# One of twelve C products of a selective scan moved from VectorE to GpSimd, and a residual matmul moved one group later

## The reference, cut to what matters

```python
def selective_scan(xs, dts, As, Bs, Cs, Dsk):
    ...
    def step(h, inp):
        u_t, d_t, B_t, C_t = inp
        dA = jnp.exp(d_t[..., None] * As)
        h = h * dA + (d_t * u_t)[..., None] * B_t[:, :, None, :]
        y = jnp.einsum('bkcn,bkn->bkc', h, C_t)
        return (h, y)
    ...
...
y = out_y[:, 0] + inv_y[:, 0] + wh_y + invwh_y
...
y = (y - mu) / jnp.sqrt(var + 1e-05) * out_norm_g + out_norm_b
y = y * jax.nn.silu(z)
return y @ out_proj_w.T
...
x = x + _L1_conv_ref(_gn(x), ...)
```

## Time and profile before

| quantity | value |
|---|---|
| median of 3 runs | 3176.9 us (3176.43 to 3177.23) |
| the profiled execution's own time | 3180.68 us |
| its span in the profile | 3177.8 us |
| granted TensorE clock, mean of the span | 0.99 |
| DVE busy in the whole span | 2619.3 us |
| POOL busy in the whole span | 2155.6 us |
| first scan of the last stage starts | 1019.93 us |

### The profile page before, as it was taken

The page is one execution under the profiler, slowest core; times in us unless marked ns, Lnnn a source line. Parts: engine busy times, 40 slices in busy tenths (PEclk is TensorE's granted clock), DMA queues, the critical chain, the costliest instruction groups (busy, mean ns, idle before and its releaser), DMA issues.

```text
span 3177.8 us, 101351 instructions
## 1 busy us (share of the span) xinstructions
PE 2769.4 (87%) x39496; PEld 2074.0 (65%) x39496; DVE 2619.3 (82%) x4161; ACT 1823.4 (57%) x3872; POOL 2155.6 (68%) x1814
## 2 busy tenths in 40 slices
PE   4999999999996788888888888888888888888876
PEld 4999999996664555656656566565665656656554
DVE  6444444445776999999999999999999999999985
ACT  1211211212224777777777777777777777777763
POOL 5333333330003988889888898888988889888883
PEclk9999999999998999999999999999999999999999
DMA  5000000002334554554545545455454554545541
GB/s 203 0 0 0 0 0 0 0 0 80 114 113 136 155 165 150 166 171 144 177 144 166 176 143 176 143 166 178 141 175 143 168 179 139 174 143 170 178 124 47
DMA packets 57086, 385.29 MB, mean 121 GB/s; under 512 B 10101, under 2 KB 15061, under 8 KB 31701
## 3 DMA queue, kind: packets, MB, share of 16 engines
q1 hardware_dynamic: 57044, 384.79, 39.2%
HBM read 352.64 MB, written 32.11 MB: 121 GB/s over the span
## 4 chain that ended last, share of the span: by engine, by line
POOL 35%; issue 28%; PE 25%; DVE 8%; ACT 2%; DMA 1%; POOLq 1%; SPq 0%; ACTq 0%; DVEq 0%
POOL arena L489 22%; PE ps L1096 10%; PE ps L1105 9%; POOL arena L462 3%; POOL arena L476 3%; POOL arena L471 3%; POOL arena L466 3%; DVE arena L772 2%; DVE arena L769 2%; PE ps L1092 2%; DVE conv_out L201 1%; PE ps L1149 1%; POOL arena L454 1%; DVE stats L565 1%; PE ps L1078 1%
## 5 line engine op out<-in xcount | busy, mean ns | idle before, releaser
L1228 PE MATMUL ps<-arena,ident 128*128 128x392 f32 (+1 forms) x4096 | 1163.0, 417 | 0.9 <-DVE arena L781 0.9
L947 ACT ACTIVATE ps<-arena,abias,a 128x390 f32<-128x390 f32 x1024 | 689.3, 677 | 314.9 <-DVE arena L772 177.1
L1228 PEld LDWEIGHTS ps<-arena,ident 128*128 128x128 f32 x4096 | 683.0, 191 | 144.1 <-DVE arena L781 1.2
L781 DVE TENSOR_TENSOR arena<-arena,ps 128x784 f32<-128x784 f32 x768 | 745.8, 971 | 26.6 <-PE ps L1218 0.3
L769 DVE TENSOR_TENSOR_SCAN arena<-ps,arena 128x392 f32<-128x392 f32 x768 | 703.2, 957 | 23.3 <-POOL arena L489 22.8
L772 DVE TENSOR_TENSOR_SCAN arena<-ps,arena 128x392 f32<-128x392 f32 x768 | 703.3, 957 | 0.0
L1218 PE MATMUL ps<-arena,sel 96*128 96x196 bf16 x3072 | 392.1, 250 | 321.1 <-DVE arena L781 321.0
L1218 PEld LDWEIGHTS ps<-arena,sel 96*128 96x128 bf16 x3072 | 230.3, 98 | 626.5 <-DVE arena L781 594.3
L489 POOL TENSOR_TENSOR arena<-arena 128x784 f32<-128x784 f32 x256 | 474.4, 1853 | 128.8 <-PE ps L1228 126.4
L951 ACT ACTIVATE ps<-arena,abias,a 128x195 f32<-128x195 f32 x1024 | 474.7, 504 | 140.0 <-DVE arena L769 72.7
L489 POOL TENSOR_TENSOR arena<-arena,wh_sb 128x784 f32<-128x784 f32 x256 | 472.8, 1853 | 69.0 <-PE ps L1228 66.9
(11 more groups left out here) (172 smaller groups left out, 3142.0 us busy)
## 6 DMA issues: line engine op xcount, KB each, us to landing
wx_sb<-b_by_state SPq DMA_DIRECT2D x64, 1568.0 KB, 6.3
wh_sb<-b_by_state SPq DMA_DIRECT2D x64, 1568.0 KB, 6.2
arena<-b_by_image SPq DMA_DIRECT2D x128, 784.0 KB, 9.1
arena<-x_seq SPq DMA_DIRECT2D x4, 2352.0 KB, 16.1
x_in<-x_pair SPq DMA_DIRECT2D x16, 588.0 KB, 4.2
x_dram<-x SPq DMA_DIRECT2D x16, 588.0 KB, 2.8
x<-x_dram SPq DMA_DIRECT2D x16, 588.0 KB, 9.9
out<-xhat SPq DMA_DIRECT2D x16, 588.0 KB, 2.8
```

Source lines behind the costliest of these rows:

```text
L781: dve.tensor_tensor(h, h, bank(3), ALU.mult).then_inc(s["readout_ready"], 1)
L947: ins = act.activation(r, src, ACT.Exp, scale=a01[:, c:c + 1], bias=abias01[:, c:c + 1])
L1228: mm = pe.matmul(ps[:, 5 if g < 8 else 6, 0:cols], ident[:, :], h[:, m * cols:(m + 1) * cols], start=(opens and m == 0), stop=(closes and ...
```

## The change

Of group 7 (`POOL_READS`) the product with C is taken from DVE's `read_out` and given to POOL as `pool_read`. POOL does it behind drive 10 of the same station (`READ_LEAD` = 3), in place in the ring buffer, when both scans of group 7 are done. It reads C from an SBUF tile, `c_chunk`, which is filled for each station by a DMA broadcast from DRAM (`spread_c`); `spill_b` writes the two states' rows there (two DMAs more). PE leaves out the spread of group 7: in the slot of group 7 it spreads group 8, in that of group 8 nothing. The sum of group 7 is done in the slot of group 10 (`BEHIND` = 2), after that of group 9, once `pool_read` is done; `ORDER` holds the order of the sums, by which `drive` now knows how many sums free its buffer. Semaphores `c_ready` and `readout_ready` rise by 2 at the group ahead of 7, so that the counts stay those of the groups. ACT's `read_bc` waits for the C spills too. Separately, the output projection's matmuls of (2, 6) move to (2, 5), and each residual matmul stands in the group next to its projection, at (2, 6), (3, 5) and (3, 7).

The diff, cut to its core:

```diff
...
 CHUNK = 16 * T
+POOL_READS = (7,)
+READ_LEAD = 3
+BEHIND = 2
 EPS = 1e-5
...
     b_by_image = nc.dram_tensor("b_by_image", [K4, 2, N, T], F32)
+    c_by_state = nc.dram_tensor("c_by_state", [K4, len(POOL_READS), 2, 2, T], F32)
     with ExitStack() as ctx:
...
         ident = sb("ident", [128, 128])
+        c_chunk = sb("c_chunk", [128, len(POOL_READS) * GC])
         sel = sb("sel", [96, N, 3, 128], BF16)
...
             "oproj_ready", "o_ready", "out_stored", "fin_z", "fin_x1",
-            "b_spilled", "b_chunk0", "b_chunk1", "b_chunk2", "skipped")}
+            "b_spilled", "b_chunk0", "b_chunk1", "b_chunk2", "skipped",
+            "c_spilled", "c_chunk_in", "pool_read")}
         convs = ((pad01, conv01_out, 2 * H + 1, par01, s["conv01_step"]), (pad2, conv2_out, H, par2, s["conv2_step"]))
...
                     lambda a: a.rearrange("p (m q t) -> p m q t", m=2, q=2))
+        def reduce_order():
+            order, late = [], []
+            for g in range(GRP):
+                if g in POOL_READS:
+                    late.append(g)
+                else:
+                    order.append(g)
+                order += [r for r in late if r + BEHIND == g]
+            return order
+        ORDER = reduce_order()
         def half_cols(hf):
...
                 sp.dma_start(b_by_image[k].rearrange("i n t -> (i n) t"), xdbl[0:2 * N, 0:T]).then_inc(s["b_spilled"], 16)
+                for q, g in enumerate(POOL_READS):
+                    for img in range(2):
+                        sp.dma_start(c_by_state[k][q, :, img, :], xdbl[N * img + 2 * g:N * img + 2 * g + 2, T:T2]
+                                     ).then_inc(s["c_spilled"], 16)
             def spread_b(P, k, j, first=False):
...
                                      ).then_inc(s["b_chunk2"], 16)
+            def spread_c(P, k, first=False):
+                sp.wait_ge(s["c_spilled"], (P + 1) * (32 * len(POOL_READS)))
+                if not first:
+                    sp.wait_ge(s["pool_read"], P * len(POOL_READS))
+                rows = c_by_state[k].rearrange("q n i t -> (q n i t)").unsqueeze(0)
+                sp.dma_start(c_chunk[:, :], rows.broadcast_to([128, len(POOL_READS) * GC])).then_inc(s["c_chunk_in"], 16)
             spill_b(0, 0)
...
                 spread_b(0, 0, j, True)
+            spread_c(0, 0, True)
             spill_xc(PAIRS - 1)
...
                         next_x(i)
+                    if ahead and max(POOL_READS) + READ_LEAD < 8:
+                        spread_c(P1, k1)
                     if ahead:
                         spread_b(P1, k1, 1)
+                    if ahead and max(POOL_READS) + READ_LEAD >= 8:
+                        spread_c(P1, k1)
                     if st == 3 and not head:
...
                 if not early:
-                    pool.wait_ge(s["reduced"], G - (RING - 1))
+                    before = st * GRP + g - RING
+                    place = before // GRP * GRP + ORDER.index(before % GRP)
+                    pool.wait_ge(s["reduced"], G - (st * GRP + g) + (place + 1))
                 src = b_chunk[g // 4][:, g % 4 * GC:(g % 4 + 1) * GC]
...
                 pool.tensor_tensor(yc, ysq, z_fin, ALU.mult).then_inc(s["gated"], 1)
+            def pool_read(P, st, g, G):
+                _, _, view = group_aps(g)
+                h = view(hb[(st * GRP + g) % RING])
+                q = POOL_READS.index(g)
+                if q == 0:
+                    pool.wait_ge(s["c_chunk_in"], P * 16 + 16)
+                pool.wait_ge(s["scan_done"], G * 2 + 2)
+                pool.tensor_tensor(h, h, view(c_chunk[:, q * GC:(q + 1) * GC]), ALU.mult).then_inc(s["pool_read"], 1)
             pool.wait_ge(s["xc_loaded"], 16)
...
                         drive(P, st, g, i * (K4 * GRP) + (st * GRP + g), head and st * GRP + g < RING)
+                        if g - READ_LEAD in POOL_READS:
+                            pool_read(P, st, g - READ_LEAD, i * (K4 * GRP) + (st * GRP + (g - READ_LEAD)))
                         if (st, g) == (2, 4) and not head:
...
                 dve.wait_ge(s["c_ready"], G + 1)
-                dve.tensor_tensor(h, h, bank(3), ALU.mult).then_inc(s["readout_ready"], 1)
+                dve.tensor_tensor(h, h, bank(3), ALU.mult).then_inc(s["readout_ready"], 1 + (g + 1 in POOL_READS))
             def pair(i, head, last):
...
                             scan(st, g, hf, G)
-                        read_out(st, g, G)
+                        if g not in POOL_READS:
+                            read_out(st, g, G)
             pair(0, True, False)
...
                     act.wait_ge(s["b_spilled"], P * 48)
+                    act.wait_ge(s["c_spilled"], P * (32 * len(POOL_READS)))
                 act.activation(xdbl[:, :], ps[:, 7, 0:T2], ACT.Copy).then_inc(s["xdbl_ready"], 1)
...
                     mm = pe.matmul(ps[:, 3 + m // 2, m % 2 * T:m % 2 * T + T], sel[:, n, kind, :], rhs, start=True, stop=True)
-                mm.then_inc(s["c_ready"], 1)
+                mm.then_inc(s["c_ready"], 1 + (g + 1 in POOL_READS))
             def reduce(st, g):
...
                 cols = GC // runs
-                opens, closes = st % 2 == 0 and g in (0, 8), st % 2 == 1 and g in (7, 11)
+                tile = [r for r in ORDER if (r < 8) == (g < 8)]
+                opens, closes = st % 2 == 0 and g == tile[0], st % 2 == 1 and g == tile[-1]
                 for m in range(runs):
...
                             pe.wait_ge(s["readout_ready"], G)
-                        spread(g, st)
-                        if not opening:
+                        if g in POOL_READS:
+                            spread(g + 1, st)
+                        elif g - 1 not in POOL_READS:
+                            spread(g, st)
+                        if not opening and (g - 1) % GRP not in POOL_READS:
                             if (st, g) == (0, 1) and not head:
...
                             reduce(*((st, g - 1) if g else ((st - 1) % K4, GRP - 1)))
+                        if g - 1 - BEHIND in POOL_READS:
+                            r = g - 1 - BEHIND
+                            pe.wait_ge(s["pool_read"], P * len(POOL_READS) + (POOL_READS.index(r) + 1))
+                            reduce(st, r)
                         if ahead and g == 0:
...
                         if not head:
-                            if (st, g) in ((0, 4), (1, 5), (2, 6), (3, 4)) and ahead:
+                            if (st, g) in ((0, 4), (1, 5), (2, 5), (3, 4)) and ahead:
                                 pe.wait_ge(s["dt_read"], P1 * 4 + 4)
...
                                 var(i - 1, g // 2 - 2)
-                            if (st, g) in ((2, 6), (3, 4), (3, 6)):
+                            if (st, g) in ((2, 5), (3, 4), (3, 6)):
                                 out_proj(i - 1, (g // 2 - 1) if st == 3 else 0)
+                            if (st, g) in ((2, 6), (3, 5), (3, 7)):
                                 residual(i - 1, (g // 2 - 1) if st == 3 else 0)
...
```

## The result

The changed kernel takes 3206.9 us in the median (3205.01 to 3207.77, 4 runs), against 3177.07 us (4 runs) for the kernel before. The ratio is 1.0093, with a 95% interval of 1.0075 to 1.011: slower by 30 us. The forecast was 3206.

The account below looks back on a forecast made before the run. DVE bounds the stage before; afterwards POOL's chain from b starts each station. 48 x (-0.03) plus 15 x 2.13, with the last station's 1.0 saved, gives +29.6: 3210.3 profiled, 3206.5 median, given as 3206; forecast 3196 to 3216 (62%), range 3168 to 3228.

Parts of the forecast that it names:

- The chain from b: Last stage: hand-off, POOL's product, delta steps to drive 0, its scan: 11.91 us against DVE's 10.93; station 33.02 against 33.05.
- b: Moment when the second scan of group 7 ends in a station, D + 21.11 us.
- the hand-off from DVE to POOL: From the end of group 7's scans to POOL's product: 0.16 us, taken from a GRU stage row; from below 0.
- The saved product: DVE's group 7 without its product saves 1.00 us a station; DVE alone would need 32.05 us.
- The affine: Third station of a pair: ACT's affine step waits 3.3 us for POOL's norm product, stalling DVE's group 3 by 2.16.
- D: Moment when a station's scan of group 0 starts on DVE.
- Rival B: POOL late, but the affine doesn't hold DVE up: 2.9 us less, 3174; with the product at 1.43, 3150; chance 14%.
- Station 0: First station of a pair: delays lie inside DVE's 0.98 us wait; group 11's spread still comes ahead of its product.
- the late centred read: First station of a pair: ACT's second centred read makes DVE meet group 9's decays some 0.7 us late.
- PE's slot of group 10: First station of a pair: spread, two sums and the skip, 4.2 us where 2.75 fit.
- the step from the profiled execution to the median: Profiled execution lies 3.8 us above the median before; taken off, 3210.3 became 3206.5.
- The product's price: POOL's new product taken at a drive's 1.81 us; from below 1.43, 24 us less in all.

Follow-up runs that it names:

- e7: Changed kernel with one more POOL instruction of about 0.55 us per station, behind drive 10 and ahead of the product: 3205.7 us (1.0086).
- e8: Changed kernel with one more POOL instruction of about 0.55 us per station, right behind the product: 3237.5 us (1.0181).
- e6: Changed kernel without any product of group 7 with C, on DVE or POOL; the sum takes the scans' result: 3128.0 us (0.9842).
- e9: Changed kernel with READ_LEAD = 4 alone: product of group 7 behind drive 11, its sum still at group 10: 3130.1 us (0.9841).
- e1: Changed kernel with the norm product on POOL behind drive 1 of station 2 in place of drive 4: 3185.8 us (1.002).
- e5: Kernel before with only the split: projection at (2, 5), residual matmul in the group after each projection: 3176.4 us (0.9996).
- e4: Changed kernel with output projection and residual matmul back together at (2, 6), (3, 4) and (3, 6): 3204.1 us (1.0081).
- e2: Changed kernel with READ_LEAD = 4 and BEHIND = 3: product behind drive 11, its sum at group 11: 3177.2 us (0.9994).

## Why the prediction was right, point by point

- **The chain from b.** Predicted 11.91 us, station 33.02; measured 33.05 to 33.08 in stations 1 and 3. The terms, at the end of station 3: the product's start to the delta steps 1.81 (predicted 1.81), from there to drive 0 8.06 (8.06), drive 0 to its scan 1.98 (predicted 1.88), and the hand-off from DVE to POOL 0.08 in the loop and 0.14 in the written-out pairs (0.16). The last two errors cancel in the loop. Both estimates came from rows outside the last stage's loop; that they were off by as much in opposite directions is luck. DVE's wait was 0.90 us on average (37.9 us in 42 waits), predicted 0.98. e7 and e8 show that this chain, and nothing else of POOL's, sets the ordinary station.
- **The saved product.** Predicted 1.00 us a station, 32.05; e6 and e9 show 32.06 and 32.08.
- **The affine.** Predicted: norm product at D + 7.17, ACT idle 3.3, stall 2.16. Measured D + 7.06, 3.10 and 1.93. Station 2: 35.05, predicted 35.18 (33.05 + 2.13; the prediction rounds it to 35.1). e1 adds what the prediction did not say: with the affine's wait gone POOL's own work is next, and only 1.2 of these 2.0 us come back. Rival B (no affine stall) would therefore have given about 3186, the time of e1, not 3174.
- **Station 0.** Here the prediction missed. It put the late centred read (0.7; measured 0.67) and PE's slot of group 10 inside the wait of 0.98, each by itself, and said that group 11's spread would still come in time. It came 0.39 us late: the centred read had also held up PE, by 0.59 us ahead of the projection in group 8's slot, and the slot of group 10 began 0.28 us after group 9's product was done. Together 1.06 us exceed what POOL's lateness covers, and station 0 took 33.19 us: 14 x 0.14 = 2 us. In e9, where POOL is on time, the same two stalls cost the whole 1.1 us in each of 15 pairs.
- **The first pair.** Three stations took 32.78 us, 0.24 less than predicted each. The trace shows the last two delta steps there 1.51 us apart where the loop has 1.58 to 1.60, drive 0 1.51 behind the last where the loop has 1.67, and the scan 1.88 behind drive 0 where the loop has 1.98. This pair is written out, with constants in its waits; the loop's hold a register. That the register makes the difference was not tried.
- **Single stalls.** The kernel before has two long stations outside the pattern, 33.66 and 40.42 us, in all 8.0 over; the changed one has other ones, 36.04, 35.88 and 36.14, in all 4.9 over the pattern. The prediction had none of this. e5 has the same two as the kernel before (33.65 and 40.32), and station 1 of the last pair is long in e1, e4, e7 and e8 too (34.9 to 36.2), so these belong to the kernels and are not chance; 36.04 does not recur in e4 or e7 and goes with a slower PE (last section). The regular part of the difference over 63 stations was thus 28.5 + 8.0 - 4.9 = 31.6 us against a predicted 30.6, and the agreement of the total to 1 us is in part luck. So is the step from the profiled execution to the median: the forecast took off the 3.8 us by which the kernel before lay above its median, 3210.3 to 3206.5, while the changed kernel's profiled execution took 3207.4 and lies 0.5 above its own. The row behind the 40.42 us is:

```profile
3035.49 1.84 DVE L769 TENSOR_TENSOR_SCAN arena<-ps,arena 128x392 f32<-128x392 f32 x2 [7.07 <-POOL arena L489]
```

The row is the scan of group 9, and the drive that it names had ended at 3018.56, 10 us before the wait began, so that drive did not end it. What did is not known.

- **The product's price.** Predicted was a drive's 1.81 us from start to start, and 1.81 came (2080.82 to 2082.63). The product itself takes 1.845 us, as the drives do, against 0.971 on DVE, 1.9 times as long. That did not decide this case: in e9 the same slow product on GpSimd (1.852 us there) brings 49 us.

## What to carry to other kernels

The following is shown by one kernel only. When work is moved to an engine with idle time, look at where in its order that idle time lies, and what stands behind the moved step's wait: a step that must wait for the bounding engine cuts the helper's lead to zero at that place, and all work between it and the next deadline becomes one exposed chain (here 11.9 us long, with drive 0 starting 1.97 us ahead of its scan where it had been 7.35). Put such a step as far behind its release as its own consumers allow (here one place, from behind drive 10 to behind drive 11, was worth 77 us), and check too that its consumer frees the buffer in time. A lead that is lost shows up at distant places: here at ScalarE, which waited 3.1 us for a product that it had not waited for before.

## What was not expected of the hardware

A stall of DVE makes PE wait, and soon after PE's return its clock can be halved: in the changed kernel the granted clock is 0.50 from 2038.50 to 2041.80 us. Busy time of each engine by stretch in station 2 of the changed kernel (length; PE, PEld, DVE, ACT, POOL; granted clock, DMA share, GB/s), and PE's timeline in the middle stretch:

```profile
2024.55:2034.55 10.00, 7.64 (x37) 4.61 (x35) 8.24 (x9) 5.04 (x10) 10.00 (x7) 1.00 0.72 202
2034.55:2044.55 10.00, 7.09 (x28) 4.16 (x28) 9.63 (x11) 9.66 (x18) 9.76 (x7) 0.83 0.51 187
2044.55:2059.59 15.04, 13.50 (x75) 10.23 (x74) 13.93 (x17) 10.61 (x23) 13.31 (x10) 1.00 0.37 91
```

```profile
2037.72 0.51 PE L1271 MATMUL ps<-arena,sel 96*128 96x196 bf16 x4 [2.91 <-DVE arena L832]
2038.07 2.48 PE L1282 MATMUL ps<-arena,ident 128*128 128x392 f32 x4
...
2046.84 1.51 PE L1282 MATMUL ps<-arena,ident 128*128 128x392 f32 x4
```

Here the lower clock begins 0.7 us after PE's wait of 2.91 us has ended (0.83 is the mean of ten microseconds), and the sum of a group takes 2.48 us in place of 1.51. The length of the wait does not decide it alone: of the 14 stations 2 in the loop of the changed kernel, each with such a wait of 2.91 to 2.94 us, nine show a lower clock (0.95 or 0.91 in the mean of the station) and five do not (1.00), and why is not known. In all but one of the nine PE has room for it; in that one (mean clock 0.91) DVE waits 1.08 us for PE, and the station takes 36.04 us. In e2 PE waits 3.75 us, and the clock falls in all 14. Five of these stations have a mean clock of 0.95 and take 34.92 to 34.94 us; nine have 0.90 or 0.91 and take 35.52 to 36.72, and in these nine alone DVE waits for PE too. One of either kind, and DVE's row in the slower one:

```profile
1877.06:1913.06 36.00, 29.47 (x135) 19.98 (x134) 31.73 (x37) 25.27 (x49) 33.09 (x21) 0.91 0.53 154
2010.08:2045.01 34.93, 27.89 (x135) 19.12 (x134) 31.73 (x36) 25.28 (x49) 33.08 (x21) 0.95 0.53 152
```

```profile
1899.43 0.97 DVE L832 TENSOR_TENSOR arena<-arena,ps 128x784 f32<-128x784 f32 x1 [1.17 <-PE ps L1271]
```

Both have the same stall of 2.8 us at group 3; the one with more time at the lower clock takes 1.07 us more. No experiment changed the clock alone, so that it is the cause is read from the traces: DVE's wait for PE stands in all nine of the slower stations and in none of the five others. So here a stall of 2.8 us, in a station that takes 32.08 without one, went with 2.8 to 2.9 us more in five stations and with 3.4 to 4.6 in nine.
